# Router stages of a two-layer transformer: order of the routing steps on VectorE and of the row scatter on GpSimd

## What is computed

```python
xln = _ln(x, ln1_w, ln1_b)
att_out = jax.nn.sigmoid(xln @ Wr) * (xln @ Wv) @ Wo
rwkv_state = xln @ Ws
x = x + att_out
h = _ln(x, ln2_w, ln2_b)
conf_r = jax.nn.sigmoid(jnp.einsum('btc,ec->bte', h, conf_rwkv))
conf_t = jax.nn.sigmoid(h @ conf_trans)[..., None]
confidences = jnp.concatenate([conf_r, conf_t], axis=-1)
difficulty = jax.nn.sigmoid(h @ w_diff)[..., None]
affinity = h @ W_aff
bids = confidences * capital_shares * difficulty + affinity
winners = jnp.argmax(bids, axis=-1)
...
out_trans = flat_h @ W1 * jax.nn.sigmoid(flat_state @ W2) @ W3
```

## Time and profile before

| | |
|---|---|
| median of 3 runs | 2365.77 us (2359.18 to 2367.14) |
| the profiled execution, its own time | 2366.78 us |
| its span in the profile | 2365.0 us |
| PE busy | 2175.2 us, 92% |
| DVE busy | 1478.8 us, 63% |
| ACT busy | 1028.0 us, 43% |
| POOL busy | 676.1 us, 29% |
| first router stage | from about 954 to 1180 us |
| second router stage | from about 1943 to 2152 us |

### The profile page before, as it was taken

How to read it: one execution, slowest core, us unless ns; L and a number is a source line. 1 busy time by engine, 2 the same in 40 slices (tenths; PEclk the granted TensorE clock), 3 DMA queues, 4 the chain that set the end, 5 groups by cost and what they waited for, 6 DMA issues and landing times. The chain is left out here.

```text
span 2365.0 us, 50326 instructions
## 1 busy us (share of the span) xinstructions
PE 2175.2 (92%) x19611; PEld 1757.4 (74%) x19611; DVE 1478.8 (63%) x3888; ACT 1028.0 (43%) x1986; POOL 676.1 (29%) x768
## 2 busy tenths in 40 slices
PE   7799999999999999899889986898999889998998
PEld 7688888888888888777689973444445457777998
DVE  2565665747565664588756647667777638885665
ACT  4344434334343434444345531555555544433554
POOL 3220110102010100356622223333333215762222
PEclk8899999999999999899999987999999999998999
DMA  7300000000000000411657755545544417114775
GB/s 243 121 19 11 11 10 11 19 2 19 2 19 11 11 2 2 136 46 65 238 183 225 225 155 110 99 82 93 90 83 81 68 40 245 55 46 135 225 224 141
DMA packets 156100, 212.87 MB, mean 90 GB/s; under 512 B 51848, under 2 KB 140192, under 8 KB 150560
## 3 DMA queue, kind: packets, MB, share of 16 engines
q1 hardware_dynamic: 141420, 190.73, 28.5%
q0 software_dynamic: 12864, 17.38, 4.4%
q10 hardware_dynamic: 1584, 1.57, 0.3%
HBM read 141.93 MB, written 67.69 MB: 89 GB/s over the span
## 5 line engine op out<-in xcount | busy, mean ns | idle before, releaser
L2438 DVE CUSTOM_DVE_ANT_0 bank<-bank,b_raw_masks 128x512 f32<-128x512 f32 (+3 forms) x512 | 239.5, 517 | 132.7 <-PE bank L2673 126.4
L2563 ACT ACTIVATE b_probsT<-bank 128x512 f32<-128x512 f32 x320 | 181.0, 602 | 177.7 <-PE bank L2673 149.0
L2152 PE MATMUL bank<-e_hT_hi,k_rwkv 128*128 128x256 f32 x1088 | 219.5, 286 | 2.8 <-DVE e_hT_lo L2056 2.8
L2152 PEld LDWEIGHTS bank<-e_hT_hi,k_rwkv 128*128 128x128 f32 x1088 | 178.1, 191 | 3.3 <-DVE e_hT_lo L2056 3.3
L2673 PE MATMUL bank<-b_k_stacked,b_q_stacked 96*128 96x512 bf16 (+3 forms) x512 | 131.0, 320 | 38.7 <-DVE b_neg_max L2438 24.4
L796 POOL TENSOR_TENSOR probs<-probs,rcp 128x512 f32<-128x512 f32 x64 | 66.8, 1043 | 346.2 <-DVE rcp L665 346.2
L2152 PE MATMUL bank<-e_hT_lo,k_rwkv 128*128 128x256 f32 x544 | 153.6, 282 | 0.0
L2166 PE MATMUL bank<-v_rwkv_hi,e_hidden_hi 128*128 (+1 forms) x544 | 152.8, 281 | 0.2 <-DVE e_hidden_lo L2077 0.2
L2166 PE MATMUL bank<-v_rwkv_lo,e_hidden_hi 128*128 (+1 forms) x544 | 152.3, 280 | 0.0
L2166 PE MATMUL bank<-v_rwkv_hi,e_hidden_lo 128*128 (+1 forms) x544 | 152.2, 280 | 0.0
L2113 ACT ACTIVATE e_relu<-bank,k_bias 128x256 f32<-128x256 f32 x272 | 113.3, 469 | 75.8 <-PE bank L2152 74.2
(11 more groups left out here) (362 smaller groups left out, 6107.7 us busy)
## 6 DMA issues: line engine op xcount, KB each, us to landing
k_rwkv<-scratch_k SPq DMA_DIRECT2D x32, 2048.0 KB, 13.5
scratch_b_parts<-b_part SPq DMA_DIRECT2D x93, 128.0 KB, 2.4
b_q_stacked<-scratch_b_parts SPq DMA_DIRECT2D x90, 128.0 KB, 4.4
b_k_stacked<-scratch_b_parts SPq DMA_DIRECT2D x90, 128.0 KB, 4.3
rows<-scratch_rows SPq DMA_DIRECT2D x34, 258.0 KB
scratch_rows<-rows SPq DMA_DIRECT2D x16, 516.0 KB, 7.7
x_tokens<-in_x_dram SPq DMA_DIRECT2D x8, 512.0 KB, 5.7
scratch_x_out<-x_tokens SPq DMA_DIRECT2D x8, 512.0 KB
```

The lines of the kernel that those rows point to most:

```text
L2152: last = nc.tensor.matmul(data[:, half * ROWS:(half + 1) * ROWS], ff.k_part(i % 2, a)[:, k, at:at + P], hT[b][:, i % 2, k], start=n == 0, ...
L2438: last = nc.vector.tensor_tensor_reduce(data[:, at:at + size], data[:, at:at + size], raw_masks[:, T - size:T], -1.0, LARGEST, ALU.add, AL ...
L2563: nc.scalar.activation(probsT[:, ring, u], fl.data("st", pair, u)[:], ACT.Exp, scale=DB ** -0.5).then_inc(fl.released("st", pair, u), 1)
```

## The change

Three moves, in `router` alone. VectorE: in turn j, `route(m)` goes behind `second_statistics(j)`, and `second_normalise(j)` goes in front of `add_third(m)` and `place(m)` in every turn. GpSimd: `scatter(m - 1)` goes between the low parts `g_lo` and `t_lo`. TensorE: `rank` of batch j - 2 is computed in turn j between `r` and `v`, instead of at the end of turn j - 1, and the bank list follows; in turns B - 1 and B the last two ranks stay where they were.

```diff
@@ order of the banks
-        order += pair("r", j) + pair("v", j) if j < B else []
+        order += pair("r", j) if j < B else []
+        order += [("rank", j - 2)] if 2 <= j < B else []
+        order += pair("v", j) if j < B else []
...
-        order += pair("w3", m) + [("rank", m)] if 0 < j < B else []
+        order += pair("w3", m) if 0 < j < B else []
+        order += [("rank", m)] if j == B - 1 else []
@@ VectorE
                     if m >= 0:
                         logits_of(m)
                         gated_third(m, (1,))
-                        route(m)
                     first_sum(j)
                     second_statistics(j)
-                    if j == B - 1:
-                        second_normalise(j)
+                    if m >= 0:
+                        route(m)
+                    second_normalise(j)
                     if m >= 0:
                         add_third(m)
                         place(m)
-                    if j < B - 1:
-                        second_normalise(j)
@@ GpSimd
             for j in range(B + 1):
                 m = j - 1
-                if j >= B - 1:
+                if j == B:
                     scatter(m - 1)
...
                 if j < B:
                     second_part(g, gT, "g_hi", "g_lo", j)
-                if j == B - 1:
-                    second_part(gt, tT, "t_hi", "t_lo", m)
-                    second_deviation(j)
-                elif j < B:
+                    if m >= 1:
+                        scatter(m - 1)
                     if m >= 0:
                         second_part(gt, tT, "t_hi", "t_lo", m)
-                    if m >= 1:
-                        scatter(m - 1)
                     second_deviation(j)
@@ TensorE (rank(m) is now a function ahead of the loop)
                     to_features(("r", j), "Wr", xT)
+                    if j >= 2:
+                        rank(j - 2)
...
                     attention()
                     if m >= 0:
                         third()
-                        rank()
+                        if j == B - 1:
+                            rank(m)
```

More of the change, by code:

```diff
@@ L1858, in _, with rank @@
                 pe.sem_inc(fl.filled("early"), 1)
+            def rank(m):
+                pe.wait_ge(s["counted"], m * 3 + 1)
+                data = begin("rank", m)
+                if m == 0:
+                    pe.wait_ge(s["consts_done"], 3)
+                nc.tensor.matmul(data[:, 0:TT], tri[:], up[:], start=True, stop=False, skip_group_check=True)
+                for t in range(1, TT):
+                    nc.tensor.matmul(data[:, t:TT], ones[:], up[:, t - 1:t].to_broadcast([P, TT - t]), start=False, stop=False,
+                                     skip_group_check=True)
+                last = nc.tensor.matmul(data[:, 0:TT], ones[:], earlier[:].to_broadcast([P, TT]), start=False, stop=True,
+                                        skip_group_check=True)
+                last.then_inc(fl.filled("rank", m), 1)
             for j in range(B + 1):
```

12 lines of the change are left out of this document (removed).

## The result

The changed kernel takes 2370.28 us (median of 20 runs, 2363.96 to 2378.35), the kernel before 2363.98 us (20 runs, 2357.44 to 2369.69). The ratio is 1.0027, 95% interval 1.0018 to 1.0036: slower by 6.3 us. That is clear of zero, but just under the 7.1 us (0.3%) from which the prediction would call it "slower"; by its own bound the outcome is "same", to which it had given 0.25. The profiled execution of the changed kernel took 2378.35 us (span 2376.4), 8 above its median. I compare by the marks and not by the spans, because the stretch between the two router stages, which the change does not touch, lasted anything from 755.6 to 770.5 us in the fourteen profiled executions of this study (first transposes of the first experts' stage to the first mark of batch 0 in the second router stage).

The account below looks back on a forecast made before the run. It took the batch period to be a ring through VectorE's program order, TensorE having spare time. Second stage +6.25 and first +4.65 gave +10.9 us, from the 2365.8 median to 2376.7; range 2362 to 2384.

Parts of the forecast that it names:

- The ring without a stall: VectorE's program order from mark to mark through att, statistics, route, rows and place: 22.1 us a batch, against 23.03 before.
- The stall: Route's small VectorE steps held beside GpSimd's two into_x additions: 1.9 us a batch, making the period 24.0.
- rival 1: Route meets only one into_x addition, stall 1.1 us a batch: +2.9 us, about 2368.7; chance 0.18.
- 2 (none): Rival: route's steps slip between the into_x additions without a stall: -8.1 us, near 2357.7; chance 0.10.
- the second meeting: A route step just behind the first held one meets the second into_x addition: 0.7 to 1.1 us lost, say 0.8.
- Second stage, +6.25: Second router stage: batches 1 to 5 add 5.0 us, batch 6 2.25, batch 7 -1.0.
- First stage, +4.65: First router stage: batches 1 and 4 +1.0 us each, 5 +1.4, 6 +2.25, 7 -1.0, 2 and 3 nothing.
- my own sum for batch 5: First stage, batch 5: 13.2 from mark to att, plus 12.6 and 1.9, gives 27.7 us against 26.3 before.
- Batch 2 hidden, 0: First stage: batches 2 and 3 end before VectorE's waits for TensorE, 4.30 and 3.05 us, which hide the change: 0.
- Scatter between the splits, nothing: GpSimd's scatter, 5.1 us, delays f_tT_lo but is covered by TensorE's spare 2 to 2.5 us a batch: no cost.
- Rank one batch later, nothing: TensorE's rank product ends about 18.2 us after the mark, place asks at about 23: no wait.
- Rival 3: TensorE's spare time runs together and its clock falls, adding some 1.5 us in ten batches: about 2391; chance 0.08 with another rival.

Follow-up runs that it names:

- e1_sum_later: Changed kernel with GpSimd's first statistics of the next batch put ahead of its two additions into x; 2355.82 us, ratio 0.997 to the kernel before.
- e2_rows_only: Kernel before with only the scatter moved between GpSimd's two splits; 2371.16 us, ratio 1.0038 to the kernel before.
- e8_second_stage: The change made in the second router stage alone, the first in the order of before; 2370.74 us, ratio 1.0039 to the kernel before.
- e3_order_only: Changed kernel with the scatter put back behind the second split on GpSimd; 2385.53 us, ratio 1.0094 to the kernel before.
- e5_sum_waits: Changed kernel with GpSimd's additions into x waiting until the routing's last small step is done; 2370.09 us, ratio 1.0037 to the kernel before.
- e7_both_edits: Changed kernel: next statistics ahead of additions into x, place behind the next gate, batch 6's additions waiting for routing's end; 2348.79 us, ratio 0.9945.

## Why the prediction was right, and where not

The direction was right, and 2370.28 lies in the range; the size, 10.9 forecast and 6.3 measured, was too large by 4.6 (of the distance to the forecast median of 2376.7, another 1.8 is that the kernel before has a median of 2363.98 over 20 runs and not 2365.8). It was built from parts, so it can be checked by parts. That the marks add up to 6.2, so near to 6.3, is partly luck: they come from one execution of each kernel, and batches 2 and 3 of the first stage vary by 1.1 and 1.4 without any change of order.

- *The ring without a stall, 22.1.* Not measured directly with this order, but e1_sum_later has it with `f_earlier` held by 0.4: 22.43 to 22.48, against 22.5. Right.
- *The stall, 1.9.* Measured 1.04 + 0.84, in exactly two steps, both ended by an addition; the period is 23.9 in batches 3 to 6 of the second stage, against 24.0 forecast. Removing the stall and nothing else from the ring (e1_sum_later) gave 1.5 a batch, 1.9 less the 0.4 above. Rivals 1 (one meeting) and 2 (none) are out. The rule cited from the Trainium skill, "SBUF — State Buffer", section "Who interferes with whom", an exclusive lock between VectorE's two-input instructions and GpSimd's reads, is borne out by the 1.21 of `f_conf`, and by 2.76 for one 128x12 step in e2_rows_only. The 1.01 belongs to `f_wc_eps`, which has one SBUF tensor and a constant, so that sentence does not cover it: the size of the second meeting came out (0.8 forecast), but the step that met it is not one of the two-input steps that the prediction counted on. A point for rival 1 was misread too: in the batch of the earlier trace rows the second reduction and the reciprocal ran at 2033.25 and 2033.66, behind the split, which ended at 2032.32, and the first reduction, at 2030.85, ahead of it; so they did not run beside it. In the changed kernel the reduction between the two long steps, at 2020.51, takes its 0.17 beside the additions and is not held.
- *Second stage, +6.25.* Measured +7.1 from mark 1 to mark 7 (forecast 7.25) and -1.0 behind mark 7 (forecast -1.0). Right in every batch but batch 2, whose 24.30 has 0.3 more.
- *First stage, +4.65: wrong.* Measured +0.2 from mark 1 to mark 7 (forecast 5.65) and -0.1 behind it (forecast -1.0). These two alone turn 10.9 into 6.2. Batches 1, 3, 4 and 6 are right (+0.9, 0, +0.9, +2.2). The failing step is the sentence on the start of `att`: "Whatever `f_xq` (L1414) gains or loses beside GpSimd's `f_gT_lo` is hidden by that". It holds in the second stage, from which it was read. In batches 2 and 5 of the first, the weight preparation runs ahead of `f_xq`, and the 13.2 from mark to `att` that I carried over unchanged for batch 5 contained the collision with `f_gT_lo`. In the changed kernel it is 10.5; with it my own sum for batch 5, 27.7, becomes 25.0, and 24.94 was measured. That takes 2.7 off: the transposes come 1.5 sooner after the mark (7.74 instead of 9.25), and the rest is the clock over the 4 us from them on, 1.00 instead of 0.65.
- *Batch 2 hidden, 0: wrong as well.* It gained 2.4, and both parts can be read. The transposes of the next input come 8.00 after the mark instead of 9.26, because the same collision stood in this batch and is gone (the preparation takes 2.48 instead of 3.80, TensorE's wait 1.07 instead of 2.33): 1.3. From there to the next mark it is 20.75 instead of 21.90, by the granted clock: 1.15. The second part is luck, not the change: e8_second_stage, in the order of before, has 20.78 there. The cover itself stayed. VectorE still waits for TensorE in this batch, 2.94 ahead of `place` and 1.13 ahead of the gate, where it waited 4.30 ahead of the gate:

```profile
1045.38 0.16 DVE L1475 TENSOR_TENSOR f_position<-bank,f_down_by 128x4 uint32<-128x4 f32 x1 [2.94 <-PE bank L1865]
```

The cover hides what VectorE loses, but not what TensorE gains, and TensorE had itself been waiting for `f_xq`. So of the 5.4 by which the first stage stayed below its forecast up to mark 7, 4.0 go with the missing collisions (2.7 in batch 5, 1.3 in batch 2), 1.15 is the clock in the profiled execution of the kernel before, and 0.3 the rest.

- *Scatter between the splits, nothing.* Right as a price in this order: TensorE waits no more than 0.33 for the second split. But e3_order_only shows what it saves there, some 16 us, and e2_rows_only what it costs in the old order, 8 us. Its price is a matter of what it pushes GpSimd's next large operation onto.
- *Rank one batch later, nothing.* Right as a price. In the second stage `place` does not wait for it. In batches 2 and 3 of the first it does, 2.94 and 1.56, which the prediction had as "No wait"; it costs nothing there, since the gate behind it waits another 1.13 for `v`, which TensorE computes after the rank.
- *Rival 3, the clock.* The granted clock stays 1.00 in batches 0 to 6 of the second stage; the spare time lies in pieces of 1.70 and 0.36. Right to be left small. In the first stage the clock mattered, but as a gain: over the 4 us from the transposes on it was 0.60 and 0.65 behind the waits of 2.33 and 2.34 in batches 2 and 5 of the kernel before, and 1.00 in the changed one, where these waits are 1.07 and 0.80.

## What to carry over

When an engine's small steps are moved, look not at what they were held by but at everything that the other engine runs in the new place, and move that too: here the same reordering was a loss beside `into_x`, and became part of a gain of 0.8% once most of the additions ran beside steps that read PSUM. A delay of the other engine's large operation is no cure if the next held step stands right behind (e5_sum_waits, e7_both_edits). And do not carry a start time from one stage to the next batch as a constant before looking at what lies in it. A wait that covers what a change costs one engine does not hide what the change saves the other. And before a batch of one profile is compared with the same batch of another, look at the granted clock in both.

## What the runs showed that was not expected

- The four normalisations (128x256, one operand in SBUF, one scalar pair per partition) are held by GpSimd's 128x512 additions: 3.37 and 3.38 in place of 1.38, and 2.10 to 2.80 where they meet the additions in part. The gate of 128x512, with one operand in PSUM and one in SBUF, is not: 1.41 beside `into_x` in e1_sum_later, as elsewhere. The section of the Trainium skill named above says that `tensor_scalar` can take both port pairs in a fast mode and then contends. The times of these steps and of `f_wc_eps` fit that; no view here shows the mode in which a step ran. The prediction used only its sentence on two inputs.
- The size of a held step does not matter: 128x1 (1.29 in place of 0.16), 128x4 (1.01) and 128x12 (2.76) all last to the end of what holds them.
- Two large operations that overlap both pay: 3.90 and 3.54 in place of 2.36 and 2.52. An indirect DMA's issue on GpSimd, mostly 0.96 to 1.11, took 1.84 to 2.30 beside the weight preparation in the changed kernel.
- Two waits of TensorE of nearly the same length, 2.54 and 2.63, in one execution: over the 4 us around the end of the first the granted clock stayed at 1.00, around the end of the second it was 0.72. Behind waits of 2.33 and 2.35 at the same place of the same order it was 0.60 in the kernel before and 1.00 in e8_second_stage. The length of the wait alone does not tell.
- With the 32 one-column matmuls of batches 2 and 3 of the first stage the granted clock fell to 0.50 in every profiled execution, for a time that made the period of batch 3 either 28.0 to 28.1 or 29.4 to 29.6, the same kernel having both.
